# A two-layer attention network on one core: the second layer's logits as row-tiled float32 matmuls instead of stacked bf16 parts

## What is computed

```
q, k, v = xf @ Wq, xf @ Wk, xf @ Wv          # 16 heads of 16 channels
s = q k^T / sqrt(16)                         # heads 0-7: mask i >= j, heads 8-15: mask i <= j
p = softmax(where(mask, s, min));  o = p v
o = concatenate([o_lb, o_la], axis=1).reshape(B, T*F, D)     # heads by rows: a regrouping
out = x + o @ Wo^T                           # everything in float32
```

## Time and profile before

| | |
|---|---|
| runs | 1825.49, 1829.11, 1841.15 us |
| the profiled execution: span | 1819.5 us |
| layer 1 in it | about 859 to 1819.5 us |
| PE busy | 1326.0 us (73%) |
| DVE, ACT, POOL busy | 917.7, 701.9, 491.3 us |
| DMA | 189.84 MB, 104 GB/s on average |

### The profile page before, as it was taken

One profiled execution on the slowest core, in us unless ns is written; L12 is line 12 of the kernel. 1 busy time (PEld: TensorE's weight loads), 2 busy tenths in 40 slices (PEclk: granted clock), 3 DMA queues, 4 the chain that ended last, 5 costly groups with the idle time before them and its releaser, 6 DMA issues.

```text
span 1819.5 us, 38881 instructions
## 1 busy us (share of the span) xinstructions
PE 1326.0 (73%) x14362; PEld 945.8 (52%) x14362; DVE 917.7 (50%) x1700; ACT 701.9 (39%) x1293; POOL 491.3 (27%) x459
## 2 busy tenths in 40 slices
PE   6477777767777677764577777878778778787775
PEld 4255555545555555544345555646556555565553
DVE  1656877777777677743243333434334333343340
ACT  2333433333444334331144443434434444444332
POOL 0033332333333333332022121212212212122120
PEclk9678988888888788877788888888888898898886
DMA  3757778877868877662757869677796786876852
GB/s 78 114 90 104 129 100 116 116 110 106 111 104 115 107 97 113 101 96 41 104 83 104 117 110 116 110 104 111 98 129 110 107 124 104 118 116 110 115 90 47
DMA packets 391383, 189.84 MB, mean 104 GB/s; under 512 B 151534, under 2 KB 374032, under 8 KB 391184
## 3 DMA queue, kind: packets, MB, share of 16 engines
q1 hardware_dynamic: 387196, 188.24, 70.9%
q10 hardware_dynamic: 4128, 0.79, 0.4%
HBM read 121.05 MB, written 67.11 MB: 103 GB/s over the span
## 4 chain that ended last, share of the span: by engine, by line
PE 25%; DMA 18%; issue 4%; ACT 3%; DVE 1%; SPq 1%; POOL 1%; DVEq 0%; ACTq 0%; POOLq 0%
DMA stack<-ct 14%; PE psC L903 5%; PE psC L919 5%; PE psA L946 3%; PE psE L1009 3%; PE psC L923 3%; PE psA L971 3%; DMA stack<-scratch_parts 2%; PE psC L990 1%; ACT probs L1033 1%; DVE cm L1100 1%; DMA scratch_parts<-parts 1%; PE psE L1001 1%; SPq L142 1%; PE psE L979 1%
## 5 line engine op out<-in xcount | busy, mean ns | idle before, releaser
L1100 DVE TENSOR_REDUCE cm<-psC 128x2 f32<-128x512 f32 (+1 forms) x384 | 253.5, 687 | 315.1 <-PE psC L923 310.9
L1144 POOL TENSOR_SCALAR_AFFINE_SELECT probs<-probs 128x1024 f32<-128x1024 f32 x128 | 139.6, 1091 | 695.8 <-ACT probs L1033 695.7
L1033 ACT ACTIVATE probs<-psC 128x512 f32<-128x512 f32 x384 | 208.2, 595 | 256.6 <-PE psC L903 256.5
L903 PE MATMUL psC<-stack 97*128 97x256 bf16 (+1 forms) x1024 | 149.4, 281 | 181.9 <-DMA stack<-ct 173.1
L690 POOL TENSOR_TENSOR probs<-probs,ebias 128x1024 f32<-128x1024 f32 x64 | 150.7, 2356 | 406.7 <-ACT probs L501 406.7
L903 PEld LDWEIGHTS psC<-stack 97*128 97x128 bf16 x1024 | 86.5, 108 | 233.8 <-DMA stack<-ct 109.4
L919 PE MATMUL psC<-stack 96*128 96x128 bf16 (+1 forms) x1024 | 166.1, 275 | 25.8 <-DMA stack<-scratch_parts 25.3
L366 PE MATMUL psA<-probs,xh 128*128 128x512 f32 x256 | 155.7, 739 | 18.4 <-DVE rest L655 12.6
L919 PEld LDWEIGHTS psC<-stack 96*128 96x128 bf16 x1024 | 94.2, 111 | 79.4 <-DMA stack<-scratch_parts 26.9
L501 ACT ACTIVATE probs<-psC 128x1024 f32<-128x1024 f32 x64 | 65.5, 1023 | 176.2 <-PE psC L403 175.5
L633 DVE TENSOR_REDUCE cm<-psC 128x8 f32<-128x512 f32 x128 | 82.3, 685 | 99.2 <-PE psC L390 98.9
(11 more groups left out here) (104 smaller groups left out, 2182.5 us busy)
## 6 DMA issues: line engine op xcount, KB each, us to landing
stack<-scratch_parts SPq DMA_DIRECT2D x768, 128.0 KB, 6.6
scratch_parts<-parts SPq DMA_DIRECT2D x64, 768.0 KB, 3.4
X<-in_xr SPq DMA_DIRECT2D x32, 256.0 KB, 3.5
scratch_heads<-on SPq DMA_DIRECT2D x64, 128.0 KB, 10.5
rows<-scratch_heads SPq DMA_DIRECT2D x32, 256.0 KB, 2.6
out<-X SPq DMA_DIRECT2D x32, 256.0 KB, 9.2
probs<-in_wop SPq DMA_DIRECT2D x1, 1024.0 KB
stack<-ct ACTq DMA_DIRECT2D x64, 8.0 KB, 7.8
```

The source lines that it names most:

```text
L903: last = nc.tensor.matmul(bank[:, n, :], stack[i.k][0:STACK + 1, 1, s.head + n, s.block * P:(s.block + 1) * P], stack[i.k][0:STACK + 1, 0, ...
L1033: nc.scalar.activation(probs[i.k][:, part * 512:(part + 1) * 512], C[0][:, part % 2 * 512:(part % 2 + 1) * 512], ACT.Exp).then_inc(exp_don ...
L1100: nc.vector.reduce_max(cm[:, s.block, s.head:s.head + s.heads], C[1][:, part % 2 * 512:(part % 2 + 1) * 512].rearrange("p (h k) -> p h k", ...
L1144: nc.gpsimd.affine_select(out=weights, in_=weights, compare_op=ALU.is_ge, fill=0.0, base=0, pattern=[[0, weights.shape[1]], [sign, P]], ch ...
```

## The change

The bf16 parts and all that belongs to them leave layer 1: the splits on ACT, DVE and POOL, the store, the twelve stack DMAs and ACT's DMA of the maxima. Instead `copy_qk` copies q and k from PSUM into `qm` and `kt` as float32 (they live in the memory of `stack`). Two heads share 32 partitions; `qm` holds q twice, once with every other head zeroed (`own` is that pattern times 1/4), so a contraction over 32 rows gives one head's logits. Each matmul names 32 partitions, and thereby one of four row tiles of the array, 32 rows by 128 columns.

A **burst** (`Burst`) is the new unit: for a tile o of eight heads and n = 0..3, `weigh_keys` makes logits by keys in banks 0 and 1 of psG from two of the row tiles, `bound_queries` makes the logits by queries of the next image in banks 2 and 3 from the two other row tiles, `lower_by_bound` adds the negated bounds in bf16 (`pick` selects the row of `ct`), and `mask_bounds` masks. Bursts n = 0, 1 have 256 columns per head, n = 2, 3 have 128. `exponent` and `take_max` now read two banks in one instruction, and the next burst writes the same banks, so it waits for both. The bounds are transposed with all 128 columns of `cm`, and lie in `ct` where they are used. `normalize` and half of `copy_qk` are on DVE. Everything is in new places of the lists; `turn` and `divide` go by halves, and the lags are (-3, 2) instead of (-2, 3).

```diff
+class Burst:
+    def __init__(self, tile, n):
+        self.tile, self.n = tile, n
+        self.at = tile * BURSTS + n
+        self.whole = n < 2
+        self.size = TOKENS if self.whole else P
+        self.weigh_rows = (0, 1) if n % 2 == 0 else (2, 3)
+        self.bound_rows = (2, 3) if n % 2 == 0 else (0, 1)
+        self.keys_of = tile if self.whole else 1 - tile
+        self.queries = slice(0, TOKENS) if self.whole else slice((1 - tile) * P, (2 - tile) * P)
+        self.queries_of = 1 - tile if self.whole else tile
+        self.keys = slice(0, TOKENS) if self.whole else slice(tile * P, (tile + 1) * P)
+        self.weigh_diagonal = tile * P if self.whole else 0
+        self.bound_diagonal = (1 - tile) * P if self.whole else 0
+BURSTS = 4
+TILE_COLS = 4 * 2 * TOKENS + 4 * 2 * P
+def prob_at(tile, whole, row):
+    return tile * TILE_COLS + (row * 2 * TOKENS if whole else 8 * TOKENS + row * 2 * P)
...
-    cm = sb("cm1", [P, TT, HEADS])
-    ct = [sb(f"ct1{k}", [HEADS, TOKENS], BF16) for k in range(2)]
+    cm = [sb(f"cm1{o}", [P, TT, P]) for o in range(CT)]
+    ct = [sb(f"ct1{o}", [P, TOKENS], BF16) for o in range(CT)]
...
+    pick = sb("pick", [P, 2, P], BF16)
...
+    weights = probs[1]
+    flat = [stack[k][:, :, :, :].rearrange("p z h t -> p (z h t)").bitcast(F32) for k in range(2)]
+    qm = [flat[k][:, 0:CT * 2 * TOKENS].rearrange("p (o e t) -> p o e t", o=CT, e=2) for k in range(2)]
+    kt = [flat[k][:, CT * 2 * TOKENS:CT * 3 * TOKENS].rearrange("p (o t) -> p o t", o=CT) for k in range(2)]
...
-            def keep_split(i):
-                wait_alone(sp, low_out, i.count(2))
-                wait_alone(sp, stacked[i.k], i.plus(-2).dmas(STACK_DMAS))
-                keep_parts(sp, i, parts, split_parts, split_out)
-            def stack_up(i):
-                wait_alone(sp, split_out[i.k], i.dmas(1))
-                wait_alone(sp, s_ready, i.plus(-2).count(LOGIT_BANKS))
-                stack_parts(sp, i, split_parts, stack, stacked)
...
-            pipeline(sp, images, [(keep_split, 2), (stack_up, 2), (store, -2), (regroup, -1), (fetch, -1)], LAGS)
...
+            pipeline(sp, images, [(lambda i: regroup(i, 0), -1), (fetch, -2), (store, -3), (lambda i: regroup(i, 1), -1)],
+                     LAGS)
...
+            def weigh_keys(i, o, n):
+                b = burst(o, n)
+                if n == 0:
+                    wait(pe, qk_out[o], i.count(QK_OPS[o]))
+                wait(pe, exp_done, i.count(ALL, b.at) if b.at else i.plus(-1).count(ALL))
+                for bank, r in enumerate(b.weigh_rows):
+                    nc.tensor.matmul(G[:, bank * 512:bank * 512 + 2 * b.size].rearrange("p (e q) -> p e q", e=2),
+                                     kt[i.k][own_rows(r), o, b.keys_of * P:(b.keys_of + 1) * P],
+                                     qm[i.k][own_rows(r), o, :, b.queries], start=True, stop=False, skip_group_check=True)
+            def lower_by_bound(i, o, n):
+                b = burst(o, n)
+                if n == 0:
+                    wait(pe, c_out[o], i.count(1))
+                for e in range(2):
+                    for bank, r in enumerate(b.weigh_rows):
+                        at = bank * 512 + e * b.size
+                        last = nc.tensor.matmul(G[:, at:at + b.size], pick[own_rows(r), e, :],
+                                                ct[o][own_rows(r), b.queries], start=False, stop=True,
+                                                skip_group_check=True)
+                        if e == 1:
+                            last.then_inc(s_ready, 1)
+            def bound_queries(i, o, n):
+                b = burst(o, n)
+                if n == 0:
+                    wait(pe, qk_out[o], i.count(QK_OPS[o]))
+                wait(pe, max_done, i.count(ALL, b.at) if b.at else i.plus(-1).count(ALL))
+                for e in range(2):
+                    for bank, r in enumerate(b.bound_rows):
+                        at = (2 + bank) * 512 + e * b.size
+                        nc.tensor.matmul(G[:, at:at + b.size],
+                                         qm[i.k][own_rows(r), o, e, b.queries_of * P:(b.queries_of + 1) * P],
+                                         kt[i.k][own_rows(r), o, b.keys], start=(e == 0), stop=False,
+                                         skip_group_check=True)
+            def mask_bounds(i, o, n):
+                b = burst(o, n)
+                for bank in (2, 3):
+                    scores = G[:, bank * 512:bank * 512 + 2 * b.size].rearrange("p (e k) -> p e k", e=2)
+                    last = nc.tensor.matmul(scores[:, :, b.bound_diagonal:b.bound_diagonal + P], identb[:, :],
+                                            (below if o else above)[:, :].unsqueeze(1).to_broadcast([P, 2, P]),
+                                            start=False, stop=True, skip_group_check=True)
+                last.then_inc(max_ready, 1)
...
-            pipeline(pe, images, [(lambda i: project_qk(i, 0), 2), (lambda i: project_qk(i, 1), 2), S(0), S(1), M(0),
-                                  M(1), S(2), S(3), W(2), M(2), M(3), S(4), S(5), W(3), M(4), M(5), S(6), S(7), M(6),
-                                  (turn_rows, -2), M(7), S(8), S(9), M(8), S(10), S(11), (output, -2), M(9),
-                                  (turn, -1), (project_v, 1), M(10), M(11), W(0), (turn_c, 1), W(1)], LAGS)
+            def B(o, n):
+                return [(lambda i: weigh_keys(i, o, n), 0), (lambda i: bound_queries(i, o, n), 1),
+                        (lambda i: lower_by_bound(i, o, n), 0), (lambda i: mask_bounds(i, o, n), 1)]
+            pipeline(pe, images, [*B(0, 0), (lambda i: project_qk(i, 1), 1),
+                                  *B(0, 1), (lambda i: weigh(i, 1), -1), (lambda i: turn_c(i, 1), 0),
+                                  *B(0, 2), (project_v, 1),
+                                  *B(0, 3), (lambda i: turn(i, 0), -1), (turn_rows, -3),
+                                  *B(1, 0), (output, -3),
+                                  *B(1, 1), (lambda i: project_qk(i, 0), 2),
+                                  *B(1, 2), (lambda i: turn(i, 1), -1), (lambda i: turn_c(i, 0), 1),
+                                  *B(1, 3), (lambda i: weigh(i, 0), 0)], LAGS)
...
+            def exponent(i, o, n):
+                b = burst(o, n)
+                wait(act, s_ready, i.count(2 * ALL, 2 * (b.at + 1)))
+                if n == 0:
+                    wait(act, pv_done[o], i.plus(-1).count(1))
+                at = prob_at(o, b.whole, b.weigh_rows[0])
+                banks = G[:, 0:1024].rearrange("p (r x) -> p r x", r=2)[:, :, 0:2 * b.size]
+                nc.scalar.activation(weights[:, at:at + 4 * b.size].rearrange("p (r x) -> p r x", r=2), banks,
+                                     ACT.Exp).then_inc(exp_done, 1)
...
+            def copy_c(i, o):
+                wait(act, c_turned[o], i.count(1))
+                wait(act, s_ready, i.plus(-1).count(2 * ALL, 2 * BURSTS * (o + 1)))
+                nc.scalar.activation(ct[o][:, :], E[:, 0:TOKENS], ACT.Copy, scale=-1.0).then_inc(c_out[o], 1)
...
-            def row_c(i):
-                wait(act, c_out, i.count(1))
-                wait(act, s_ready, i.plus(-2).count(LOGIT_BANKS))
-                act.dma_start(stack[i.k][STACK:STACK + 1, 0, :, :], ct[i.k][:, :]).then_inc(c_row[i.k], 16)
...
+            pipeline(act, images, [(lambda i: copy_outputs(i, 0), -1), X_(0, 0), X_(0, 1),
+                                   (lambda i: copy_outputs(i, 1), -1), (lambda i: copy_c(i, 1), 0), X_(0, 2), (copy_v, 1),
+                                   X_(0, 3), (copy_rows, -3), X_(1, 0), X_(1, 1), (copy_qk, 2), X_(1, 2),
+                                   (lambda i: copy_c(i, 0), 1), X_(1, 3)], LAGS)
...
+            def take_max(i, o, n):
+                b = burst(o, n)
+                wait(dve, max_ready, i.count(ALL, b.at + 1))
+                if n == 0:
+                    wait(dve, c_turned[o], i.plus(-1).count(1))
+                banks = G[:, 1024:2048].rearrange("p (r x) -> p r x", r=2)[:, :, 0:2 * b.size]
+                first = b.bound_rows[0]
+                nc.vector.reduce_max(cm[o][:, b.queries_of, :].rearrange("p (r x) -> p r x", x=COL)[:, first:first + 2, 0:2],
+                                     banks.rearrange("p r (e k) -> p r e k", e=2), AX_X).then_inc(max_done, 1)
...
+            def normalize(i):
+                wait_alone(dve, proj_v, i.plus(-2).count(1))
+                wait_alone(dve, proj_qk[1], i.plus(-2).count(1))
+                for c in range(CT):
+                    nc.vector.tensor_scalar(xh[i.k][:, c, :], X[:, bass.ds(i.index(), 1), c, :].rearrange("p i t -> p (i t)"),
+                                            rs_y[:, bass.ds(i.index(), 1), c], shift[:, bass.ds(i.index(), 1), c],
+                                            ALU.mult, ALU.add).then_inc(xh_done, 1)
...
```

(2 more changed lines are left out.)

## The result

The changed kernel takes 1640.75 us (median of four runs, 1622.35 to 1650.19) against 1833.72 us for the kernel before (median of four runs): a ratio of 0.893, with a 95% interval of 0.886 to 0.900. The profiled execution has a span of 1620.6 us; it is the fastest of its four runs. Layer 0, which the change leaves alone, ended 11 us earlier in it than in the profile before, and single executions of either kernel spread by about 1% about their medians. So I compare layer 1 by its steps, the mean of the 31 from the first image's first exp to the last image's.

A forecast was written before the change was run, and what follows sets the result against it. Layer 1 was taken as bound by PE behind one DMA. A step: 27.83 - 5.88 - 3.1 + 2.5 + 0.2 + 1.0 + 0.8 = 23.4 us; 1819.5 - 137 - 26 = 1656.5 span, 1665 us median; 8 in 10: 1600 to 1805.

The forecast's parts named there:

- The waits, -5.88: Layer 1: PE's waits for the row of maxima and the stacked parts go, 5.88 us a step less.
- The clock comes back: Layer 1: without long waits PE's clock stays at its upper level, 3.1 us a step less (0 to 3.6).
- The bursts, 9.5 for 7.0: PE in layer 1: eight bursts take 9.5 us a step, replacing scores, bounds and masks of 7.0; +2.5 us.
- Switches, +1.0: PE: 18 switches between tile shapes a step instead of 8, 0.1 us each; +1.0 us a step (0 to 2).
- Hand-overs, +0.8: PE waiting at bursts for exp or maxima, nearly all covered by other work; +0.8 us a step (0 to 3).
- The additions together: Layer 1 step: bursts +2.5, turn_c +0.2, switches +1.0 and hand-overs +0.8, together +4.5 us.
- Start, -18: Layer 1 from xh to first exp: 28 us instead of 46.6, 18 less (0 to 25).
- End, -8: From the last image's first exp to the end, 44.7 us before: 8 less (0 to 15).
- partial overlap: Rival: row tiles overlap only in part, or the clock still falls at times; 1715 to 1790 us, chance 22%.
- the 2150 of the rival: Rival: row tiles do not overlap, bursts take 25.1 us a step; 2150 us, chance 9%.

The follow-up runs named there:

- before_no_parts: The kernel before with layer 1's store and twelve stack DMAs, and the waits for them, left out; splits and row DMA stay: 1567.71 us (0.864), step 20.23.
- mask_first: The changed kernel with mask_bounds ahead of lower_by_bound in every burst, same matmuls: 1691.68 us (0.933), step 24.37.
- uncovered: The changed kernel with the third burst directly behind the second, weigh and turn_c moved after it: 1673.31 us (0.912), step 23.66.

## Why the prediction was right, and where it was not

The forecast of 1665 us is 1.5% above the median, its step 23.4 against 22.36, and the mechanism is the one forecast: the waits go, the clock comes back, row tiles overlap. Two terms were wrong in opposite directions, the clock by 1.4 us a step and the additions by 2.4, so part of the closeness is luck.

- **The waits, -5.88: right.** None of them is left in layer 1, and nothing new took their place (0.2 us a step on ACT). before_no_parts shows the cause, the store and the stack DMAs.
- **The clock comes back: right. The term, -3.1: mis-sized, it was 1.7.** The kernel before without its DMAs runs at clock 1.00 with a step of 20.23, so the low clock had cost 27.83 - 5.88 - 20.23 = 1.7. The working took one step for all. Two waits of the kernel before, each with the time behind it (columns as in the earlier trace rows), the first that of the earlier trace rows:

```profile
1302.10:1307.80 5.70, 0.00 (x0) 0.01 (x1) 0.69 (x1) 0.60 (x1) 0.00 (x0) 0.96 1.25 144
1307.80:1318.00 10.20, 10.19 (x90) 6.83 (x91) 4.70 (x7) 6.17 (x12) 4.49 (x5) 0.69 0.27 41
1331.10:1337.10 6.00, 0.00 (x1) 0.01 (x1) 0.69 (x1) 0.60 (x1) 0.00 (x0) 0.79 1.25 138
1337.10:1347.30 10.20, 10.05 (x96) 6.86 (x97) 5.34 (x8) 7.17 (x14) 5.42 (x5) 0.79 0.30 43
```

In the step that the working used, the low stretch lay almost wholly behind the wait; in the next, and in most of the 31, it began within the wait, where it costs nothing. Over all 31 steps the granted clock of the trace gives 3.5 us lost a step, of which 2.2 while PE was busy. Why these 2.2 cost 1.7 stays open.
- **The bursts, 9.5 for 7.0: the sum right, the order in them wrong.** I had the first record of bound_queries 0.43 behind weigh_keys, and lower_by_bound hidden beneath it: 1.29 + 0 + 0.22. In fact the first records of all four tiles go out together, and lower_by_bound is in the open: 0.96 + 0.32 + 0.22. The totals, 1.51 and 1.50, agree by chance; the small burst is 0.98, not 0.87. Counted from start to start of PE's records over all 31 steps, bursts take 10.3 us a step, not 9.5, and what they replace took 8.1, not 7.0: scores 3.4, bounds 2.7, masks 2.1, measured in before_no_parts at clock 1.00. Both sizes were low by about the same, so the difference, +2.1, is near the +2.5.
- **Switches, +1.0: the price nearly right** (0.125 instead of 0.1, mask_first), the count not: the traces show 6 changes of tile shape a step before and 19 after, not 8 and 18. Most of them are in the 10.3 of the bursts already.
- **Hand-overs, +0.8: too much.** PE waits 6.1 us in 700, 0.2 a step, because what stands between bursts covers nearly all of them; uncovered shows 1.3 for one that is not.
- **The additions together: +4.5 forecast, 22.36 - 20.23 = +2.1 measured.** Counted in the same way in the changed kernel and in before_no_parts, these are +2.1 for bursts instead of logits, +0.4 for turn_c, -0.4 for weigh, +0.5 for projections, output and transposes (the tile shape changes behind more of them now), and -0.5 of idle time of PE, 0.2 a step after against 0.7 in before_no_parts.
- **Start, -18: it was 16.2.** From xh to the first exp it is 30.4 us instead of 46.6, against 28 forecast. **End, -8: it was 1.6.** The timeline of the changed kernel's end:

```profile
1577.57 1.02 ACT L1071 ACTIVATE probs<-psG 128x1024 f32<-128x1024 f32 x1 [0.68 <-PE psG L928]
...
1595.44 5.02 PE L973 MATMUL psA<-probs,va 128*32 128x256 f32 x64
1595.58 0.60 ACT L1071 ACTIVATE probs<-psG 128x512 f32<-128x512 f32 x1 [1.77 <-PE psG L928]
...
1606.35 0.36 SPq L885 DMA_DIRECT2D scratch_heads<-on  x1
```

The last bursts took 18.0 us, not 15, and from the last exp to the last regroup it is 10.8, not 6: with nothing of a next image to do PE was busy 14.51 of the 17 us before 1595, the granted clock is 0.55 from 1595.5 to 1600.5, and weigh of both tiles takes 5.02 us, where half of it, 32 records, takes 1.51 in a full step (1222.20 to 1223.71).

Of the rivals, partial overlap (1715 to 1790) is what two tiles at a time would have been: 1781. That the change could lose at all was not far-fetched: with one tile at a time it takes 2644, worse than the 2150 of the rival, because the clock falls as well; with all rows and no overlap, at clock 1.00, it takes 2104.

## What to carry to other kernels

A wait's releaser can be just the last DMA to land, and not the cause: take the DMAs in flight with it away before you rebuild the one that is named. When a clock that fell is to be priced, count the low stretches only where the engine is busy, and over many steps, not one. Small float32 matmuls that are independent went side by side on row tiles here when they were issued next to each other, at 3.6 to 3.7 times the rate for four tiles; count what else can ride there for nothing (here the bounds' float32 half), and keep matmuls over all rows out of the middle. And if a small-tile kernel can only keep one tile at work, expect less than its busy share says.

## What the hardware did that I had not expected

- With one tile of 32 rows at a time TensorE was busy 594.95 of 600 us and was granted 0.70 of its clock, down to 0.50 inside bursts. With two tiles at work it was 0.99, with the same columns over all 128 rows 1.00. Why the rows matter to the gate no run shows.
- Records of weigh_keys and bound_queries go out mixed: half of each from 1217.27 and 1217.28 on, the other half at 1217.80 and 1217.82, though in the program all of weigh_keys stands ahead. Each tile has 0.86 us of work, and the four together take 0.96. Weight loads of 128 columns into different row tiles start together as well, where loads into the whole array in layer 0 took 0.114 us each.
- A change of tile shape costs some 0.1 us here, and it can pass for the cost of the work ahead of it: weigh_keys alone holds PE for 1.06 us and, with the bounds on the two other tiles, for 0.96, but for 1.08 when the next matmul has 128 rows there too. From first start to last end its own records take 1.12 us with the bounds (1217.27 to 1217.80 + 0.59) and 1.13 without.
